# First attention of a two-layer attention and expert kernel: unrounded fp32 products in place of three rounded terms

## The reference, cut to what matters

```python
x = layer_norm(x, ln_m_g, ln_m_b); lat = layer_norm(latents, ln_l_g, ln_l_b)
q = lat @ Wq
kv = jnp.concatenate([x, lat], axis=1) @ Wkv
k, v = jnp.split(kv, 2, axis=-1)
dots = jnp.einsum('bhid,bhjd->bhij', q, k) * scale
attn = jax.nn.softmax(dots, axis=-1)
out = jnp.einsum('bhij,bhjd->bhid', attn, v)
return out @ Wout
```

## Time and profile before

| what | value |
|---|---|
| time, median of 3 runs | 792.21 us (791.63 to 795.18) |
| profiled execution, span from its first to its last instruction | 788.3 us |
| PE busy | 706.3 us (90%) |
| DVE busy | 475.7 us (60%) |
| ACT busy | 378.0 us (48%) |
| POOL busy | 377.4 us (48%) |
| mean granted TensorE clock | 0.948 of full |

### The profile page before, as it was taken

How to read it: one execution, slowest core, us unless ns; L and a number is a source line. 1 busy time by engine, 2 the same in 40 slices (tenths; PEclk the granted TensorE clock), 3 DMA queues, 4 the chain that set the end, 5 groups by cost and what they waited for, 6 DMA issues and landing times.

```text
span 788.3 us, 13872 instructions
## 1 busy us (share of the span) xinstructions
PE 706.3 (90%) x4810; PEld 430.8 (55%) x4810; DVE 475.7 (60%) x966; ACT 378.0 (48%) x580; POOL 377.4 (48%) x361
## 2 busy tenths in 40 slices
PE   4899999999999999999999999997995687568991
PEld 3654555545556555556545545566995343336661
DVE  4745484585585875667477478465443386845553
ACT  4475554564654554655445444344552643223440
POOL 7264453473464475444464553634333304674552
PEclk9999999999999999999999999998998697569996
DMA  9999999990000000000030004301212500122325
GB/s 253 197 201 197 204 190 10 4 4 1 1 1 2 1 14 1 1 1 1 1 121 2 1 1 108 114 24 32 72 32 80 155 1 28 35 75 69 88 66 177
DMA packets 109867, 50.62 MB, mean 64 GB/s; under 512 B 44804, under 2 KB 103048, under 8 KB 109800
## 3 DMA queue, kind: packets, MB, share of 16 engines
q1 hardware_dynamic: 106280, 42.46, 36.0%
q0 software_dynamic: 3520, 7.27, 2.7%
HBM read 20.07 MB, written 29.64 MB: 63 GB/s over the span
## 4 chain that ended last, share of the span: by engine, by line
PE 74%; DVE 11%; issue 5%; ACT 3%; POOL 3%; DMA 2%; another core or an unknown queue 1%; SPq 1%; DVEq 0%; POOLq 0%; ACTq 0%
PE PSUM L1631 14%; PE PSUM L1663 13%; PE PSUM L1598 5%; PE PSUM L1463 5%; PE PSUM L1498 4%; PE PSUM L1468 4%; PE PSUM L1729 4%; PE PSUM L1423 3%; PE PSUM L1425 2%; PE PSUM L1424 2%; PE PSUM L1612 2%; PE PSUM L1605 2%; PE PSUM L1649 2%; PE PSUM L1693 2%; DVE REC L1377 1%
## 5 line engine op out<-in xcount | busy, mean ns | idle before, releaser
L866 ACT ACTIVATE PT<-PSUM 128x1024 f32<-128x1024 f32 x128 | 128.6, 1024 | 134.1 <-PE PSUM L1631 133.7
L690 POOL TENSOR_TENSOR PSUMS<-PT 128x1024 f32<-128x1024 f32 x32 | 76.0, 2376 | 210.4 <-ACT PT L866 171.4
L690 POOL TENSOR_TENSOR PSUMS<-PSUMS,PT 128x1024 f32<-128x1024 f32 x62 | 149.6, 2413 | 16.8 <-ACT PT L866 9.9
L1254 DVE TENSOR_REDUCE TOPS<-PSUM 128x2 f32<-128x1024 f32 x128 | 152.1, 1220 | 6.9 <-PE PSUM L1598 6.5
L1663 PE MATMUL PSUM<-PT,BIG 128*64 128x512 f32 x512 | 130.6, 611 | 0.0
L1209 DVE TENSOR_TENSOR SIL<-SIL,PSUM 128x256 f32<-128x256 f32 (+1 forms) x62 | 32.2, 519 | 65.7 <-ACT SIL L783 46.8
L1244 DVE TENSOR_TENSOR KL<-PSUM,KH 128x512 fp32r<-128x512 f32 x32 | 22.1, 691 | 68.2 <-ACT KH L844 67.7
L1598 PE MATMUL PSUM<-KH,QH 64*128 64x512 f32 x256 | 57.9, 449 | 4.0 <-DVE QL L1247 3.7
L1663 PEld LDWEIGHTS PSUM<-PT,BIG 128*64 128x64 f32 x512 | 28.4, 135 | 53.4 <-issue 52.0
L1598 PEld LDWEIGHTS PSUM<-KH,QH 64*128 64x128 f32 x256 | 24.2, 183 | 59.2 <-DVE TOPS L1254 24.9
L783 ACT ACTIVATE SIL<-PSUM 128x256 f32<-128x256 f32 (+1 forms) x62 | 28.6, 462 | 56.7 <-PE PSUM L1463 31.4
(11 more groups left out here) (256 smaller groups left out, 1365.5 us busy)
## 6 DMA issues: line engine op xcount, KB each, us to landing
lists_d<-EMPTY SPq DMA_DIRECT2D x3, 2730.0 KB, 35.3
lists_b<-EMPTY SPq DMA_DIRECT2D x3, 2470.0 KB, 33.4
lists_d<-EMPTY SPq DMA_DIRECT2D x1, 2665.0 KB, 34.9
XG<-lists_d SPq DMA_DIRECT2D x39, 65.0 KB
lists_b<-EMPTY SPq DMA_DIRECT2D x1, 2405.0 KB, 17.2
BIG<-in_L_ffn_w SPq DMA_DIRECT2D x1, 2048.0 KB
W2ALL<-in_L_ffn_w SPq DMA_DIRECT2D x4, 512.0 KB, 6.2
PT<-results_d SPq DMA_DIRECT2D x8, 256.0 KB, 4.4
```

The source lines that it names most:

```text
L690: pool.tensor_tensor(PSUMS[:, i % 2], PTT[:, i % 2, 0] if kt == 1 else PSUMS[:, i % 2], PTT[:, i % 2, kt], ALU.add).then_inc(s_ps, 1)
L866: act.activation(PTT[:, i % 2, kt], PSUM[:, place:place + 2, :], ACT.Exp, scale=DH ** -0.5).then_inc(s_exp, 1)
L1254: dve.tensor_reduce(TOPS[:, c, 0, :], PSUM[:, place:place + 2, :], AX.X, ALU.max).then_inc(s_max, 1)
```

## The change

Projections, values and scores of the first attention become single fp32 products. `three`, `WH`, `WL`, `XTH`, `XTL`, `CTH`, `CTL`, `KL` and `QL` go, with the instructions that made them. The weights are read where they were loaded (`WA`), the features as `XF`. Rounded `QH` (ScalarE) and `KH` (now VectorE) remain for the maxima alone; the scores read `QF` (ScalarE, which existed) and a new `KF` (VectorE). The step with `MINUS` and `TOPROW` stays fp32r. The bank of the queries is released by `QF`, the bank of the keys by `KF`, each by itself. `QF` is now read by the last pair's scores, so the gate weights of the expert that lies there load after them.

```diff
-            def three(dst, aH, aL, bH, bL):
-                pe.matmul(dst, aH, bH, start=True, stop=False)
-                pe.matmul(dst, aH, bL, start=False, stop=False)
-                return pe.matmul(dst, aL, bH, start=False, stop=True)
...
                     for n in range(2):
-                        c = slice(n * BANK, (n + 1) * BANK)
-                        last = three(PSUM[:, place + n, :], XTH[:, k, cols], XTL[:, k, cols], WH[:, 2, c], WL[:, 2, c])
+                        last = pe.matmul(PSUM[:, place + n, :], XF[:, k, cols], WA[:, 2, n * BANK:(n + 1) * BANK], start=True, stop=True)
...
-                    for w in range(2):
-                        last = three(PSUM[:, place + w, :], WH[:, w, c], WL[:, w, c], XTH[:, k, :], XTL[:, k, :])
-                    last.then_inc(s_qk, 1)
-                    release(mine, (s_qkl, 2 * a + 2))
+                    for w, made in enumerate((s_qp, s_kp)):
+                        pe.matmul(PSUM[:, place + w, :], WA[:, w, c], XF[:, k, :], start=True, stop=True).then_inc(made, 1)
+                    release(mine[0:1], (s_qf, a + 1))
+                    release(mine[1:2], (s_kf, a + 1))
                 elif name == "top":
...
                     if c == 0:
-                        pe.wait_ge(s_qkh, 3 * i + 2)
+                        pe.wait_ge(s_qh, i + 1)
+                        pe.wait_ge(s_kh, i + 1)
...
-                    for step in range(4):
-                        if (kt, step) == (0, 3):
+                    for step in range(2):
+                        if (kt, step) == (0, 1):
                             pe.wait_ge(s_toprow, i + 1)
...
-                            lhs = (KH[r, k, c], KL[r, k, c], KH[r, k, c], MINUS[r, :])[step]
-                            rhs = (QH[r, k, :], QH[r, k, :], QL[r, k, :], TOPROW[r, i % GROUP, :])[step]
-                            last = pe.matmul(PSUM[:, place + h, :], lhs, rhs, start=step == 0, stop=step == 3)
+                            lhs = (KF[r, k, c], MINUS[r, :])[step]
+                            rhs = (QF[r, i % GROUP, :], TOPROW[r, i % GROUP, :])[step]
+                            last = pe.matmul(PSUM[:, place + h, :], lhs, rhs, start=step == 0, stop=step == 1)
...
                     act.activation(QH[:, a % 2, :], PSUM[:, place, :], ACT.Copy).then_inc(s_qh, 1)
...
-                    dve.wait_ge(s_qkh, 3 * a + 2)
-                    dve.tensor_tensor(KL[:, a % 2, :], PSUM[:, place + 1, :], KH[:, a % 2, :].bitcast(F32),
-                                      ALU.subtract).then_inc(s_qkl, 1)
-                    dve.wait_ge(s_qkh, 3 * a + 3)
-                    dve.tensor_tensor(QL[:, a % 2, :], PSUM[:, place, :], QH[:, a % 2, :].bitcast(F32), ALU.subtract).then_inc(s_qkl, 1)
+                    dve.wait_ge(s_kp, a + 1)
+                    if a >= 2:
+
+                        dve.wait_ge(s_sc, scores_of(a - 2))
+                    dve.tensor_copy(KH[:, a % 2, :], PSUM[:, place + 1, :]).then_inc(s_kh, 1)
+                    dve.tensor_copy(KF[:, a % 2, :], PSUM[:, place + 1, :]).then_inc(s_kf, 1)
...
             sp.wait_ge(s_sc, context_of(2 * B - 1))
-            gates_of(0, E - 1)
+            gates_of(0, GROUP - 1)
+            gates_of(GROUP, E - 1)
 
             sp.wait_ge(s_sc, len(scored))
+            gates_of(GROUP - 1, GROUP)
             gates_of(E - 1, E)
```

More of the change, by code:

```diff
@@ L157, in build, with sb1 @@
         with ExitStack() as first:
-            def sb1(name, *shape):
-                return first.enter_context(nc.sbuf_tensor(name, [P, *shape], F32R))
-            WH = sb1("WH", 3, INNER)
-            WL = sb1("WL", 3, INNER)
-            XTH = sb1("XTH", 2, S)
-            XTL = sb1("XTL", 2, S)
-            QH = sb1("QH", 2, S)
-            QL = sb1("QL", 2, S)
-            KH = sb1("KH", 2, S)
-            KL = sb1("KL", 2, S)
+            def sb1(name, *shape, dt=F32):
+                return first.enter_context(nc.sbuf_tensor(name, [P, *shape], dt))
+            WA = sb1("WA", 3, INNER)
+            XF = sb1("XF", 2, S)
+            QH = sb1("QH", 2, S, dt=F32R)
+            KH = sb1("KH", 2, S, dt=F32R)
+            KF = sb1("KF", 2, S)
         W2ALL = sb("W2ALL", E * F_B)
@@ L259, in build @@
         s_tr = sem("lane_turned")
-        CTD = Steps(sem("ctx_dve"), ["ct", "low", "raw"])
-        s_cth = sem("ctx_high")
-        XTD = Steps(sem("features_dve"), ["feat", "low"])
-        s_xth = sem("features_high")
-        s_wh, s_wl = sem("weights_high"), sem("weights_low")
+        CTD = Steps(sem("ctx_dve"), ["ct", "raw"])
+        s_xf = sem("features")
         s_const_r = sem("rounded_consts")
@@ L768, in keep_weights @@
                 if j == 0:
-                    act.wait_ge(ld_w1, 48)
+                    act.wait_ge(ld_w1, 80)
                 if j >= 2:
@@ L838, in scalar_program @@
                 elif name == "qk":
-                    act.wait_ge(s_qk, a + 1)
+                    act.wait_ge(s_qp, a + 1)
                     if a >= 2:
-                        act.wait_ge(s_sc, scores_of(a - 2))
-                    act.activation(QH[:, a % 2, :], PSUM[:, place, :], ACT.Copy).then_inc(s_qkh, 1)
-                    act.activation(KH[:, a % 2, :], PSUM[:, place + 1, :], ACT.Copy).then_inc(s_qkh, 1)
+                        act.wait_ge(s_top, TOPS_OF * (a - 1))
+                    act.activation(QH[:, a % 2, :], PSUM[:, place, :], ACT.Copy).then_inc(s_qh, 1)
                     if a >= GROUP:
                         act.wait_ge(s_sc, context_of(a // GROUP - 1))
-                    act.activation(QF[:, a % GROUP, :], PSUM[:, place, :], ACT.Copy).then_inc(s_qkh, 1)
+                    act.activation(QF[:, a % GROUP, :], PSUM[:, place, :], ACT.Copy).then_inc(s_qf, 1)
                 elif name == "max_turn":
@@ L859, in scalar_program @@
                         act.wait_ge(s_ps, 3 * (i - 1))
-                    if i < 2 and kt == 0:
-                        act.wait_ge(s_wl, 3)
                     if i == 1 and kt == 0:
@@ L1537, in context_keys @@
                     c = slice(pr * P, (pr + 1) * P)
-                    last = three(PSUM[:, 7 - part, pr % GROUP * P:(pr % GROUP + 1) * P], WH[:, 1, c], WL[:, 1, c], CTH[:, :], CTL[:, :])
+                    last = pe.matmul(PSUM[:, 7 - part, pr % GROUP * P:(pr % GROUP + 1) * P], WA[:, 1, c], CT, start=True, stop=True)
                 last.then_inc(s_kc, 1)
                 free[7 - part] = s_kcf, part + 1
-            pe.wait_ge(s_cth, 1)
-            pe.wait_ge(*CTD.at(0, "low"))
-            pe.wait_ge(s_wl, 1)
+            pe.wait_ge(*CTD.at(0, "ct"))
+            pe.wait_ge(ld_wk, 16)
             context_keys(0)
-            turn_nrm(RUN_OF["a", 0], 6, XTD.at(0, "feat"))
+            turn_nrm(RUN_OF["a", 0], 6, (s_xf, 1))
             for name, a, place, banks in order_a:
@@ L1568, in tensor_program @@
                         ctx_b = slice(b * M, (b + 1) * M)
-                        for step, weights in enumerate((WH, WL)):
-                            for p in range(GROUP):
-                                last = pe.matmul(
-                                    PSUM[p * M:(p + 1) * M, place + b // 2, b % 2 * 2 * P:(b % 2 + 1) * 2 * P].rearrange("p (g n) -> p g n", g=2),
-                                    CT[:, ctx_b], weights[:, 2, :].bitcast(F32).rearrange("p (g q n) -> p g q n", g=2, q=GROUP)[:, :, p, :],
-                                    start=step == 0, stop=step == 1)
+                        for p in range(GROUP):
+                            last = pe.matmul(
+                                PSUM[p * M:(p + 1) * M, place + b // 2, b % 2 * 2 * P:(b % 2 + 1) * 2 * P].rearrange("p (g n) -> p g n", g=2),
+                                CT[:, ctx_b], WA[:, 2, :].rearrange("p (g q n) -> p g q n", g=2, q=GROUP)[:, :, p, :],
+                                start=True, stop=True)
                     last.then_inc(s_vctx, 1)
@@ L1733, in tensor_program @@
                 elif name == "a_turn":
-                    turn_nrm(RUN_OF["a", a], place, XTD.at(a, "feat"))
+                    turn_nrm(RUN_OF["a", a], place, (s_xf, a + 1))
                     release(mine, free[place])
```

77 lines of the change are left out of this document (18 added, 59 removed).

## The result

The changed kernel takes **822.86 us** (median of 4 runs, 821.16 to 825.60), the kernel before 791.92 us in the same job: ratio 1.0383, 95% interval 1.0347 to 1.0419. 827 was forecast, with 817 to 857 as the range. The profiled run took 821.16 us, its span is 819.4.

What follows compares the result with a forecast made beforehand. TensorE was taken to set the pace; 19.8 + 15.3 - 1.8 + 1.8 - 0.5 = 34.6 us on 792.2 gave 827 us, range 817 to 857.

Steps and rivals of the forecast that it cites:

- TensorE sets the pace: In the 32 pairs TensorE is busy 473.2 of 477.3 us; ScalarE and VectorE have slack, relieving them buys only few waits.
- Scores, +19.8: 128 scores steps on TensorE: one fp32 product of 0.86 us replaces three fp32r terms of 0.705, +0.155 each, +19.8 us.
- A change of type is free: Switching between fp32 and fp32r at the same tile sizes on TensorE costs nothing beyond the passes; upper bound 0.25 us a step.
- Projections and values, +15.3: Two fp32 products (1.72 us) replace six fp32r (1.38) a step, +0.34; 45 of 48 steps counted, +15.3 us.
- Context's values, -1.8: The context's values were two fp32 products for one, 3.66 us in the chain; half goes, -1.8 us.
- `KH` waits, net +1.8: `KH` in VectorE's queue delays a pair's first `top` 1.1 us, the 0.75 wait for `QL` goes; five places, +1.8 us.
- Start, -0.5: First projections no longer wait 1.4 us for the features' split, but products at 1.2 GHz add 0.9; -0.5 us kept.
- Later gate loads, nothing: One more expert's gates load after the last scores step, covered by work before the first expert tile; costed at nothing.

Runs made afterwards that it cites:

- experiment 4: Changed kernel with the product `KF,QF` of every scores step made twice, the second overwriting the first; 928.7 us in a single run.
- experiment 3: Changed kernel with `KH` made by ScalarE, no longer by VectorE; 803.1 us beside 780.9 for the kernel before, ratio 1.0302.
- experiment 2: Kernel before with only the scores changed to one fp32 product and the `TOPROW` term, `KH` still on ScalarE; 793.4 us beside 780.9, ratio 1.0152.
- experiment 9: Changed kernel with the first quarter of a group's reciprocals moved behind `KH`, `KF` and the first maximum; 824.1 us, ratio 1.0375 to the kernel before.
- experiments 6 and 7: Changed kernel with two unread 128 x 1024 VectorE subtractions added at the start, operands both in SBUF, then one in PSUM; 815.5 and 814.1 us.
- experiment 10: Kernel of experiment 8 with the first quarter of a group's reciprocals moved behind `KL`, `QL` and the first maximum; 798.1 us beside 794.5, ratio 1.0035.
- experiment 8: Kernel before, three terms kept, context's values and half its keys single fp32 products, weights' subtractions after GpSimd's power; 778.8 us beside 780.6, ratio 0.9970.

## Why the prediction was right, step by step

- **TensorE sets the pace.** Right, and shown: 0.86 us more of product in a step gives 0.86 us more of time (experiment 4), and in experiment 3 PE is busy 503.5 of 503.7 us.
- **Scores, +19.8.** Measured +19.2 from start to start; in experiment 2, where the waits for `QL` go with them, the stretch grew by 14.5. The step of 0.705 against 0.86 was sized right.
- **A change of type is free.** Right for the two directions together (experiment 4). With one direction free by the earlier trace rows, the other is too.
- **Projections and values, +15.3.** Measured +13.7. Per step it is 0.32 and not 0.34, and I counted 45 steps after the start where 43 are: five of the 48 lie ahead of the first scores step.
- **Context's values, -1.8.** Measured -1.7.
- **`KH` waits, net +1.8.** Five waits, 5.6 us in all, up to 1.2 each, in place of 3.7 us for `QL`: +1.9. The place, the count and the size were right. The cause as I put it, the reciprocal in front, was only the neighbour: with the reciprocal moved away the maxima came late instead (experiment 9), and with `KH` moved to ScalarE nothing did (experiment 3). What I didn't forecast is that a version without any such wait was at hand, 6.2 us faster.
- **Start, -0.5.** Measured -2.3, the term that was mis-sized. I counted the split that went off the path (15.34 - 13.9) and took the features' own time as fixed. It was not: they came at 11.57 in place of 13.09, and GpSimd's `NMR`, which they wait for, ended 1.52 us earlier too, since GpSimd was no longer held up by the subtractions (experiments 6 and 7, and `NMR`). That is 1.5 of the 1.8 us missed; the rest is no more than the start moves by itself, 29.0 and 29.5 us for the same changed kernel.
- **Later gate loads, nothing.** The rest of the span is 1.2 us longer, where two profiles of the changed kernel differ by 6.8 in it; no wait for those weights stands in PE's list. Not tested alone.

The errors (scores -0.6, projections -1.6, context and `KH` +0.1 each, start -1.8, rest +1.2, all else -0.9 by the stretch's own 32.2) sum to -3.5: 34.6 was forecast and 31.1 measured on the spans. The mechanism was right; that the total came out within 3.5 us is in part luck, since the rest of the span, costed at nothing, moves by more than that between profiles of one kernel.

Two readings of the prediction are to be set right. It gave the clock as at its upper level through the first 27 slices; that is what the row says, but terms of 0.42 us in the first slice, which the prediction uses itself, are at the lower level, so the row doesn't show the start's clock. And it looked for 0.86 us from one `QF,KF` record to `TOPROW`; the profile shows 0.46, by the early start of that record, and only the sum of 1.10 can be checked.

## What to carry to other kernels

Price a product by start to start at the very sizes of the kernel: here three fp32r terms (0.70 us for two heads and 512 columns) are cheaper than one fp32 product (0.86), so in this kernel fp32 paid only where it also took away a product, as in the context's values. An engine with 40% of idle time can still be late in single places; try to move work off its queue there, to an engine that is free in the same microseconds, and not only to change its order. When a change takes work away from VectorE, look what GpSimd does beside it.

## What I had not expected of the hardware

- One VectorE subtraction of 128 x 1024 with both operands in SBUF (1.22 us) that starts 0.08 us ahead of a GpSimd instruction on 4 columns lengthens it from 1.05 to 2.05 us, and one of 0.20 us to as much as 1.18. Two GpSimd instructions that lie wholly inside one with an operand in PSUM keep their 0.31 us.
- A `TOPROW` record behind fp32 products has a length of 0.80 us and begins with the second pair of their records, against 0.40 behind fp32r ones, though the step as a whole is the plain sum of its products. Read such a step from its first start to the next group's.
- The moment at which TensorE's products become twice as fast moves the first scores step by about as much as the change does. In the profile of experiment 10 the terms of the values at 21 us still take 0.42 us each, in that of experiment 8 those at 20 us take 0.23, and the first scores steps are at 32.4 and 30.0 us; the first projections are at 14.37 and 14.15, and the instructions are the same up to there. The granted clock of both stretches reads 1.00 in the profile, so the level (1.2 GHz, then 2.4) can be read only from the lengths.
